# Column-wise scale and bias, queries from the PSUM bank, and centering on ScalarE in a perceiver layer

## The reference

```python
# x (2,64,256) latents, ctx (2,1024,256), mask (2,1024), all float32 but the mask
def _layernorm(x, eps=1e-5): return (x - mean(x)) / sqrt(var(x) + eps)

def xattn(ctx, lat, ...):                       # 16 heads of 64
    xn = layernorm(ctx) * ln_x_g + ln_x_b
    ln = layernorm(lat) * ln_l_g + ln_l_b       # lat is _layernorm(x)
    q = ln @ Wq
    k, v = concat([xn @ Wkv, ln @ Wkv]) split in two      # 1088 keys for each batch
    qn = q / rms(q per head) * qn_g / 8;  kn = k / rms(k per head) * kn_g
    return softmax(mask(qn @ kn.T)) @ v @ Wout + bout

x = x + xattn(ctx, _layernorm(x), ...)
x = x + attn(_layernorm(x), ...)                # pairs of latents, 16 heads
x = x + ffn(_layernorm(x), ...)                 # entmax gate, two low-rank layers, gelu
```

## Time and profile before

| | us |
|---|---|
| median of 3 runs | 239.11 (238.82 to 239.4) |
| the profiled execution | 238.49 |
| its span, first to last instruction | 236.7 |
| PE busy in it | 224.9 (95%) |
| DVE busy | 153.8 (65%) |
| ACT busy | 149.7 (63%) |
| POOL busy | 80.7 (34%) |

### The profile page before, as it was taken

One profiled execution on the slowest core, in us unless ns is written; L12 is line 12 of the kernel. 1 busy time (PEld: TensorE's weight loads), 2 busy tenths in 40 slices (PEclk: granted clock), 3 DMA queues, 4 the chain that ended last, 5 costly groups with the idle time before them and its releaser, 6 DMA issues.

```text
span 236.7 us, 4203 instructions
## 1 busy us (share of the span) xinstructions
PE 224.9 (95%) x1475; PEld 194.5 (82%) x1475; DVE 153.8 (65%) x346; ACT 149.7 (63%) x329; POOL 80.7 (34%) x127
## 2 busy tenths in 40 slices
PE   7588999999999999999999999999999998999994
PEld 6364887886788989888898989899999987999883
DVE  1779999998887876967767655566675530312541
ACT  4255589888886869686766567778777655015141
POOL 5368876773473647464250500000000010100200
PEclk9799999999999999999999999999999999999999
DMA  6875101100000000000000799600000000000000
GB/s 176 303 214 216 47 24 28 42 25 22 0 25 0 0 6 0 0 0 3 0 0 3 264 424 322 151 3 0 0 4 0 0 4 0 0 3 0 0 3 22
DMA packets 11236, 13.80 MB, mean 58 GB/s; under 512 B 1584, under 2 KB 9936, under 8 KB 10960
## 3 DMA queue, kind: packets, MB, share of 16 engines
q1 hardware_dynamic: 10944, 13.01, 16.9%
q10 hardware_dynamic: 272, 0.52, 0.6%
HBM read 13.14 MB, written 0.13 MB: 56 GB/s over the span
## 4 chain that ended last, share of the span: by engine, by line
PE 71%; DVE 13%; ACT 4%; issue 3%; DMA 3%; POOL 2%; SPq 1%; ACTq 0%; DVEq 0%; POOLq 0%
PE banks L1158 19%; PE banks L1025 14%; PE banks L1072 9%; PE banks L1101 8%; PE banks L1287 5%; DVE small L784 4%; PE banks L1179 4%; DMA rows<-in_L_xattn_ln_x_b 3%; PE banks L1172 3%; DVE sk L796 3%; PE banks L1103 2%; PE banks L1210 2%; PE banks L1312 1%; DVE raw L752 1%; DVE small L791 1%
## 5 line engine op out<-in xcount | busy, mean ns | idle before, releaser
L819 DVE TENSOR_TENSOR ptl<-banks,pth 128x512 fp32r<-128x512 f32 (+1 forms) x48 | 26.8, 558 | 26.2 <-ACT pth L578 25.3
L1158 PE MATMUL banks<-xnh,pth 128*128 128x256 f32 x128 | 37.6, 294 | 0.0
L1158 PE MATMUL banks<-xnh,ptl 128*128 128x256 f32 x128 | 36.3, 283 | 0.0
L1158 PE MATMUL banks<-xnl,pth 128*128 128x256 f32 x128 | 36.2, 283 | 0.0
L578 ACT ACTIVATE pth<-banks 128x512 fp32r<-128x512 f32 (+1 forms) x48 | 23.7, 494 | 10.3 <-PE banks L1025 9.2
L461 POOL TENSOR_TENSOR small<-small 128x16 f32<-128x16 f32 x7 | 20.4, 2908 | 27.3 <-DVE small L791 27.3
L525 ACT ACTIVATE sk<-banks 128x512 f32<-128x512 f32 x36 | 20.6, 606 | 14.2 <-PE banks L1072 14.1
L796 DVE TENSOR_TENSOR sk<-banks,small 128x512 f32<-128x512 f32 x36 | 23.0, 679 | 6.9 <-POOL small L461 6.9
L784 DVE TENSOR_REDUCE small<-sk 128x8 f32<-128x512 f32 x36 | 23.6, 679 | 5.3 <-ACT sk L525 5.1
L442 POOL COPY sp<-sp 128x64 f32<-128x64 f32 x16 | 4.1, 254 | 62.8 <-ACT sp L559 62.8
L1158 PEld LDWEIGHTS banks<-xnh,pth 128*128 128x128 f32 x128 | 24.5, 192 | 0.4 <-issue 0.4
(11 more groups left out here) (177 smaller groups left out, 480.9 us busy)
## 6 DMA issues: line engine op xcount, KB each, us to landing
knT<-in_L_attn_qkv_kernel SPq DMA_DIRECT2D x1, 3072.0 KB, 12.1
raw<-in_ctx SPq DMA_DIRECT2D x16, 128.0 KB, 2.1
knT<-in_L_xattn_Wq SPq DMA_DIRECT2D x1, 1024.0 KB, 9.2
wv<-in_L_xattn_Wkv SPq DMA_DIRECT2D x1, 1024.0 KB, 5.1
wout_sb<-in_L_xattn_Wout SPq DMA_DIRECT2D x1, 1024.0 KB, 5.5
knT<-in_L_attn_out_kernel SPq DMA_DIRECT2D x1, 1024.0 KB, 15.6
wraw<-in_L_xattn_Wkv ACTq DMA_DIRECT2D x1, 512.0 KB, 4.2
wraw<-in_L_xattn_Wkv SPq DMA_DIRECT2D x1, 512.0 KB, 6.1
```

Of the source, the lines that this page charges most:

```text
L819: nc.vector.tensor_tensor(ptl[:, j0:j1, :], banks[:, t3_bank(u, c), 0:(j1 - j0) * P].rearrange("p (j r) -> p j r", j=j1 - j0), pth[:, j0:j ...
L1158: nc.tensor.matmul(banks[:, u_bank(u), 0:D], p_[:, j, :], x_, start=(j == 0 and i == 0), stop=False)
```

## The change

Four things. (1) The scale and bias of both layer norms come in as eight short rows of 128 (`gb8`), which TensorE transposes into columns and ScalarE copies to `gcols`; for the latents and the first context tile TensorE transposes the centered data, and ScalarE applies scale and bias per partition while it copies from the bank (`scaled`), once as the high part and once in full (`lnTf`, `x0Tf`). The row form of the latents, still needed for the values, is computed later by GpSimd. (2) The DMAs of ln_l_g and ln_l_b as rows move behind context tile 3, those of ln_x_g and ln_x_b behind tile 1, the query weights behind tile 2, the latents' copies and the value weights behind tile 7. (3) Tiles k = 1 to 11 are centered by ScalarE with scale rstd and bias -mean x rstd, for which GpSimd computes one more small value. (4) The queries are scaled from the bank into `qbd` in `keys_out`, in four pieces, and `qT` with the later pieces goes. The mask piece moves from item 4 to 6, `lnhl` from item 3 to 7.

```diff
 (sync)
-            sp.dma_start(gl, row(ln_l_g)).then_inc(w_lrows, 16)
-            sp.dma_start(bl, row(ln_l_b)).then_inc(w_lrows, 16)
+            for i, v in enumerate((ln_l_g, ln_l_b)):
+                sp.dma_start(*gain_rows(i, v)).then_inc(w_cols, 16)
...
+                if k == 4:
+                    sp.wait_ge(xt_ps, 2)
...
+                if k == 1:
                     sp.dma_start(rows[:, 0, :], row(ln_x_g)).then_inc(w_rows, 16)
                     sp.dma_start(rows[:, 1, :], row(ln_x_b)).then_inc(w_rows, 16)
-                if k == 1:
+                if k == 2:
                     sp.dma_start(wq_sb, wq_v).then_inc(w_q, 16)
                 if k == 3:
+                    sp.dma_start(gl, row(ln_l_g)).then_inc(w_lrows, 16)
+                    sp.dma_start(bl, row(ln_l_b)).then_inc(w_lrows, 16)
...
-                if k == 4:
+                if k == 7:
                     sp.wait_ge(ln_ready, 1)
 (gpsimd)
-                rsqrt_var(mv[:, k % 4, :], ve[:, k % 4:k % 4 + 1], rstd[:, k % 4:k % 4 + 1], 1e-5).then_inc(rstd_ready, 1)
+                last = rsqrt_var(mv[:, k % 4, :], ve[:, k % 4:k % 4 + 1], rstd[:, k % 4:k % 4 + 1], 1e-5)
+                if centered_by_act(k):
+                    link(last)
+                    last = nc.gpsimd.tensor_scalar(nmr[:, k % 4:k % 4 + 1], mv[:, k % 4, 0:1], -1.0, rstd[:, k % 4:k % 4 + 1],
+                                                   ALU.mult, ALU.mult)
+                last.then_inc(rstd_ready, 1)
...
-                if i == 0:
+                if i == 1:
+                    pool.wait_ge(lat_hat, 1)
+                    pool.wait_ge(w_lrows, 32)
+                    link(nc.gpsimd.tensor_tensor(lmul, latg, gl, ALU.mult))
+                    nc.gpsimd.tensor_tensor(lnf, lmul, bl, ALU.add).then_inc(ln_ready, 1)
+                if i == 2:
                     pool.wait_ge(w_gain, 64)
 (scalar)
+            for i, v in enumerate((ln_x_g, ln_x_b)):
+                act.dma_start(*gain_rows(2 + i, v)).then_inc(w_cols, 16)
+            def tile_center(k):
+                act.wait_ge(rstd_ready, k + 1)
+                nc.scalar.activation(raw[:, k % 4, :], raw[:, k % 4, :], ACT.Identity, bias=nmr[:, k % 4:k % 4 + 1],
+                                     scale=rstd[:, k % 4:k % 4 + 1]).then_inc(xhat_ready, 1)
+            def scaled(dst, n):
+                for c in range(DC):
+                    g = 2 * DC * n + c
+                    last = nc.scalar.activation(dst[:, c, :], banks[:, t1_bank(n), c * P:(c + 1) * P], ACT.Identity,
+                                                bias=gcols[:, g + DC:g + DC + 1], scale=gcols[:, g:g + 1])
+                return last
 (keys_out)
-                    ins = nc.scalar.activation(qT[:, h, :], bank, ACT.Copy)
+                    act.wait_ge(qg_ready, 1)
+                    act.wait_ge(zeroed, 1)
+                    pairs = qbd[:, :, :].rearrange("p (b g) i -> p b g i", b=B)
+                    for e in range(2):
+                        e0, e1 = e * DH, (e + 1) * DH
+                        ins = nc.scalar.activation(pairs[e0:e1, :, 4 * h:4 * h + 4, e * M:(e + 1) * M],
+                                                   bank[e0:e1, :].rearrange("p (g b i) -> p b g i", g=4, b=B), ACT.Copy,
+                                                   scale=qg[e0:e1, 3:4])
 (scalar, order)
-            xt_high(0)
-            nc.scalar.activation(lnTf, banks[:, t1_bank(0), 0:D].rearrange("p (c r) -> p c r", c=DC),
-                                 ACT.Copy).then_inc(lnT_ready, 1)
+            act.wait_ge(cols_ps, 1)
+            nc.scalar.activation(gcols, banks[:, 6, 0:4 * DC], ACT.Copy).then_inc(cols_ready, 1)
+            act.wait_ge(cols_ready, 1)
+            act.wait_ge(xt_ps, 1)
+            scaled(xth[:, 0], 0).then_inc(xth_ready, 1)
+            scaled(lnTf, 0).then_inc(lnT_ready, 1)
             wk_high(1)
             squares(0, 0)
-            xt_high(1)
+            act.wait_ge(xt_ps, 2)
+            scaled(xth[:, 1], 1).then_inc(xth_ready, 1)
+            scaled(x0Tf, 1).then_inc(x0T_ready, 1)
             squares(0, 1)
+            tile_center(1)
             context_high(0)
...
-                    if 5 <= i < 9:
-                        queries(*divmod(i - 5, 2))
                     context_high(i)
+                if i == 1:
+                    tile_center(2)
                 act.wait_ge(n2_ready, i + 1)
                 nc.scalar.activation(sd[:, i % 2, :], n2[:, i % 2, :], ACT.Sqrt).then_inc(sd_ready, 1)
+                if i > 1:
+                    tile_center(i + 2)
                 if i + 2 != QI and i + 2 <= ITEMS_A:
                     xt_high(tile(i + 2))
-                if i in (4, 9):
+                if i == 1:
+                    tile_center(3)
+                if i in (6, 9):
...
-                if i == 3:
+                if i == 7:
                     act.wait_ge(w_lat, 16 * 2 * B)
 (vector)
-            nc.vector.scalar_tensor_tensor(latg, xb[:, :], lmv[:, 0:1], gl, ALU.subtract, ALU.mult).then_inc(lat_hat, 1)
-            nc.vector.scalar_tensor_tensor(lnf, latg, lrs, bl, ALU.mult, ALU.add).then_inc(ln_ready, 1)
+            center(latg, xb[:, :], lmv[:, 0:1], lrs).then_inc(lat_hat, 1)
...
-                else:
-                    tile_center(i + 2)
 (tensor)
-            keep_clock(10, 7)
+            keep_clock(9, 3)
+            pe.wait_ge(w_cols, 64)
+            nc.tensor.transpose(banks[:, 6, 0:4 * DC], gb8, ident[0:4 * DC, 0:4 * DC]).then_inc(cols_ps, 1)
             norm_transposed(0)
+            keep_clock(4, 3)
```

More of the change, by code:

```diff
@@ L113, in perceiver_layer @@
         gl = early(4, 0, D)
+        gb8 = early(2, 0, P)[0:8, :]
+        lmul = early(2, D, D)
+        x0Tf = early(2, 2 * D, D).rearrange("p (c r) -> p c r", c=DC)
         bl = early(4, D, D)
@@ L116, in perceiver_layer, with centered_by_act @@
         wq_sb = knT[:, 1, 5:5 + DC, 0:INNER]
+        def centered_by_act(k):
+            return 1 <= k <= FA + 3
         def item(n):
@@ L142, in perceiver_layer @@
         mcol = small[:, 202:203]
+        gcols = small[:, 204:212]
+        nmr = small[:, 212:216]
         b0keys = knT[:, 0, :, :].rearrange("p g n -> p (g n)")
@@ L180, in perceiver_layer @@
         w_lrows = sem("w_lrows")
+        w_cols = sem("w_cols")
+        cols_ps = sem("cols_ps")
+        cols_ready = sem("cols_ready")
+        x0T_ready = sem("x0T_ready")
         z1_ready = sem("z1_ready")
@@ L216, in perceiver_layer @@
         qg_ready = sem("qg_ready")
-        qbd_ready = sem("qbd_ready")
         s_ps = sem("s_ps")
@@ L341, in perceiver_layer, with gain_rows @@
         logits_ps = banks[:, 3:6, :].rearrange("p a n -> p (a n)")[:, 0:KW]
+        def gain_rows(i, v):
+            return gb8[i * DC:(i + 1) * DC, :], v.rearrange("(c p) -> c p", p=P)
         def row(v):
@@ L544, in keys_out @@
                 ins.then_inc(kt_ready, 1)
[L546 to L555, removed]
             def exponentials(u):
@@ L776, in xt_low @@
                 dve.wait_ge(xth_ready, n + 1)
+                full = banks[:, t1_bank(n), 0:D].rearrange("p (c r) -> p c r", c=DC)
                 if n == 0:
                     dve.wait_ge(lnT_ready, 1)
-                nc.vector.tensor_tensor(xtl[:, n % 2, :, :], banks[:, t1_bank(n), 0:D].rearrange("p (c r) -> p c r", c=DC),
-                                        xth[:, n % 2, :, :].bitcast(F32), ALU.subtract).then_inc(xtl_ready, 1)
+                    full = lnTf
+                if n == 1:
+                    dve.wait_ge(x0T_ready, 1)
+                    full = x0Tf
+                nc.vector.tensor_tensor(xtl[:, n % 2, :, :], full, xth[:, n % 2, :, :].bitcast(F32),
+                                        ALU.subtract).then_inc(xtl_ready, 1)
             def key_norm2(i, h):
@@ L855, in _ @@
             wk_low(0)
+            xt_low(0)
             tile_center(0)
-            xt_low(0)
             wk_low(1)
@@ L861, in _ @@
             xt_low(1)
-            tile_center(1)
             key_norm2(0, 1)
@@ L867, in _ @@
                     key_norm2(i, 1)
-                if i > 0:
+                if i > 1:
                     tile_mv(i + 3)
                 key_clamp(i)
-                if i == 0:
-                    tile_stats(2)
-                else:
-                    tile_center(i + 2)
+                if i <= 1:
+                    tile_stats(i + 2)
                 dve.wait_ge(sd_ready, i + 1)
@@ L884, in _ @@
                     xt_low(tile(i + 2))
-                if i == 0:
-                    tile_center(2)
-                    tile_stats(3)
-                    tile_sums(4)
+                if i == 1:
+                    tile_stats(4)
+                    tile_sums(5)
             key_norm2(ITEMS_A, 0)
@@ L1030, in norm_transposed @@
                     pe.wait_ge(consts, 1)
-                    pe.wait_ge(ln_ready, 1)
-                    src = lnf
+                    pe.wait_ge(lat_hat, 1)
+                    src = latg
```

(14 more changed lines are left out.)

4 lines of the change are left out of this document (removed).

## The result

The changed kernel takes 242.57 us (242.32 to 243.08, 4 runs) against 238.98 (4 runs): ratio 1.0150, 95% interval 1.0128 to 1.0172, 3.6 us slower. The forecast was slower, at 240.2, with a range up to 241.9; the time lies above it. The profiled execution took 242.66, its span 240.8, against 238.49 and 236.7. In it root(10), the last event of stage A, comes at 62.06 instead of 57.80, 4.26 later, so all of the loss is in stage A, where it was looked for.

The account below looks back on a forecast made before the run. Bound: the ScalarE-VectorE loop in stage A. Root(4) +0.25, then 24.95 against 24.12 to root(10), +0.83: in all +1.1, 239.6 on the profiled execution, 240.2 on the median. Range 237.6 to 241.9.

Parts of the forecast that it names:

- the loop that bounds the kernel: Stage A: root, centering, key copies, squares, reductions, clamp through ScalarE and VectorE; plain rounds of 3.91, chance 0.50.
- Opening: Start of stage A: rows land at 9.3, GpSimd's first operation ends at 10.5, rstd(4) ready at 24.6.
- Centering on ScalarE: Behind each root, not hidden in idle time: 0.40 a round, bounds 0.31 and 0.52.
- Queries straight from the bank: Round ending at root(4): four pieces with a pointer take 2.3 in place of 0.95, bounds 2.0 and 2.5.
- The bare length of the loop: Stage A round without centering, read from one round: 3.49, of which 2.16 from first square to next root.
- ScalarE waits for GpSimd: At tile 4's centering, ScalarE arrives at about 21 and waits until 24.6; TensorE's item 4 starts at 25.4.
- the 0.02 of gaps: Added to each plain round of stage A, making 3.89 into 3.91.
- TensorE as bound: Stage A rival: TensorE's 3.85 an item sets the pace, extras hidden, 238.0 us; chance 0.25.
- Cancelled: Stage A rival: queries 2.0, centering 0.31, rstd(4) at 24.3, root(10) at 57.6, 238.9 us; chance 0.13.
- the slower rival: Opening: rows no earlier than 11.16, or granted clock at half while TensorE waits for tile 1; 241.8 us, chance 0.12.
- The 0.8: Later end than forecast if centering didn't overlap the next operation at all, with rounds of 4.0.
- The rule of the Trainium skill on GpSimd's SBUF interfaces: Low parts of latents and tile 0: each could hold GpSimd some 0.3 more, left out of the sum.

Follow-up runs that it names:

- e13: Changed kernel without clamp, centering of k = 4 to 11 on VectorE, queries scaled later, latents at item 5, value weights behind tile 13: 236.25 us, ratio 0.9872.
- e12: Changed kernel with centering as a plain copy and query pieces scaled by a constant, so no pointer operands: 241.44 us, ratio 1.0092.
- e1: Changed kernel with centering of tiles k = 4 to 11 back on VectorE: 239.68 us, ratio 1.0011 to the kernel before.
- e7: Kernel before with only the centering of tiles k = 4 to 11 on ScalarE, and GpSimd's extra value: 241.74 us, ratio 1.0101.
- e2: Changed kernel with queries copied out first and scaled in four later pieces (items 5 to 8), as before: 240.86 us, ratio 1.0074.
- e3: Changed kernel with GpSimd's subtraction for tiles k = 3 to 9 cut from 256 to 8 columns: 241.36 us, ratio 1.0082.
- e8: Changed kernel without VectorE's clamp in stage A, the root taken straight from the summed squares: 240.14 us, ratio 1.0028.
- e6: Changed kernel with centering of k = 4 to 11 on VectorE, queries scaled later, latents' GpSimd operations at item 5: 238.63 us, ratio 0.9972.
- e14: As e13, with the latents' two GpSimd operations one each at items 4 and 5: 235.37 us, ratio 0.9844 to the kernel before.
- e4: Changed kernel with the latents' two GpSimd operations at item 5 instead of item 1, lnhl at item 9: 242.98 us, ratio 1.0158.

## Why the prediction was wrong

The direction was right, and so was the loop that bounds the kernel; its bare length, which was taken for a constant, was not, and that is the step that failed. Root(10) was forecast at 58.9 and came at 62.06, 3.2 later. Term by term:

- *Opening.* Rows landed 9.84 (9.3 forecast), the first GpSimd operation ended 11.14 (10.5), rstd(4) with its added value was ready at 25.28 (24.6). +0.7. The 14.1 us between the last two was met. In other executions of kernels with the same queue up to there the rows landed as late as 11.5 (e13), so this DMA term deserved a wider bound.
- *Centering on ScalarE.* 0.50 from start to start, 0.40 forecast, eight times: +0.8. The step took one pointer's cost (0.08) for an operation with two. In e12 it is 0.59 with both and 0.40 without; Identity became Copy in the same edit, but the query pieces, a Copy in both, give 0.09 for one pointer, so two pointers account for the 0.19. That the operation is not hidden was right (e1, e7).
- *Queries straight from the bank.* 2.79, 2.3 forecast, +0.5. The upper bound of 2.5 was too low as well: four pieces follow each other with no overlap, 0.68 each plus gaps, where the earlier trace rows had 0.721 and the step took 0.58 apart. e2 confirms the cost of the round, 6.08 against 4.38.
- *The bare length of the loop.* This is the step that failed most: the 3.49, and in it the 2.16 from first square to root. 2.16 from first square to root was read from a round in which the clamp had taken 0.17. In the changed kernel the clamps took 0.21, 0.43, 0.54, 0.54, 0.30, 0.30 and 0.55, then 0.17, and first square to root took 2.19, 2.41, 2.53, 2.52, 2.28, 2.28, 2.54 and 2.14: +1.6. The prediction had put collisions with GpSimd into the difference between rounds of 4.02 and a loop of 3.49, and then reckoned the changed kernel at 3.49 and the centering, so they were at nothing. But they grew: with GpSimd set off by ScalarE's centering, the subtraction meets the clamp in every plain round (the 3.44 and 3.67 above). Two parts of the change bring this about together: in e2 and e7 centering is on ScalarE too, but the query pieces stand at items 5 to 8 and hold the subtraction back, and there the clamps take 0.17 or 0.18. e3 shows the cause and the price of the collisions, 1.6 us; e8 that of the whole clamp, 2.9. How the meeting comes about is read from the traces, not tested by a run of its own, and e6, with a mean of 350 and centering on VectorE, shows that there are other ways to it.
- *ScalarE waits for GpSimd* at the centering of tile 4 was right (a wait of 1.04, forecast over 3; root(2) itself came later than reckoned, at 24.05 and not 21, since centering of tile 3 already waited 2.3 for GpSimd, a wait that the prediction had not reckoned). For tile 5 no wait was left, -0.3. Item 4 on TensorE started at 27.68, not at 25.4, since its key transposes also waited 1.14 for ScalarE's key copies; that cost nothing at root(4), as item 4's squares stood behind the query pieces until 32.89.

These sum to 3.3; the 0.02 of gaps that the forecast gave each of its plain rounds were not there, -0.1, which makes the 3.2. The median of the timed runs is 3.6 us longer, the profiled pair 4.2 apart.

The rivals: TensorE as bound is out, it waited 5.7 us for copies. "Cancelled" is out. In the profiled execution the rows came early and the granted clock stayed at 1.00 from 10 to 58 us, so neither of the causes of the slower rival applied, though its time was the nearest. The rule of the Trainium skill on an ACTIVATE's length ("ScalarE: Activation LUTs", Rules for kernel authors, 0.51 estimated for 256 elements) was under the 0.59 of the profile; it prices a pointer for the bias, and here a second stands for the scale. The 0.8 that the prediction drew from it is what centering did add, but by luck: 0.59 long with 0.09 overlapped, not 0.51 with none. The rule of the Trainium skill on GpSimd's SBUF interfaces, shared with VectorE ("GPSIMD Engine Reference", Specifications), was weighed in the wrong direction: it was used for GpSimd being held by VectorE, and what cost 1.6 us was a VectorE operation held by GpSimd. The rule names VectorE instructions in a 2-port perf mode too, which the prediction left out; the clamp has one tensor input, and no run here shows its mode.

## What to carry to other kernels

Before work is moved from one engine to another, find the loop that runs through all engines once per round, and whether the receiver is idle at the very place in its order where the work is put; idle time elsewhere doesn't help. Read the bare length of such a loop from several rounds, and list for every short VectorE operation in it what GpSimd runs beside it: when one operation of the loop sets off both engines, as the centering does here, whether they meet is the same in every round, and one small operation more or less decides it. And a lead won at the start reaches the end only if each later wait is looked at in turn; here it took a load and two GpSimd operations moved (e13, e14).

## What the runs showed of the hardware

- A VectorE operation of 128x16 float32 in SBUF took 0.17 us alone and up to 0.73 beside a GpSimd tensor-tensor operation of 128x256, ending within 0.04 of that one's end (39.63 and 39.59; 29.26 and 29.23 in e4). With the GpSimd operation 8 columns wide the mean was 0.191 (e3).
- The other way round, that GpSimd operation took 0.73 alone and 1.16 when it met the low half of the second weight cast on VectorE (9.33 to 10.56), ending 0.58 after it.
- ScalarE took 0.40 for a Copy of 128x256 in SBUF without pointer operands (e12) and 0.59 for an Identity with scale and bias as pointers (the changed kernel); for a Copy of 64x512 from PSUM 0.59 with a constant scale and 0.68 with a scale pointer.
- The same broadcast load, at the same place of the same queue, landed 6.1 (e2) to 7.9 us (e13) after its issue in different executions.
- The granted clock was 0.50 from 9 to 12 us in the kernel before, after TensorE had waited 1.7 us for the latents; in the changed kernel, where that wait was gone, it was 1.00 over the same stretch.
